# Six of eight norms' last step on GpSimd, row sums of the banded softmax on VectorE, and new order lists

## The chip, the cores and the metric

The kernel runs on one core of one Trainium2 chip. The metric is the device time of one launch in microseconds (us). Of the kernel before, three runs gave 1738.55, 1740.66 and 1747.6 us; the median is 1740.66 us. Everything is one program with hand-placed semaphores: TensorE (PE), VectorE (DVE), ScalarE (ACT), GpSimd (POOL) and the DMA queue of SyncE (SP) each work through a list of their own, in order.

## The reference, cut to what matters

Eight batches of 512 tokens by 128 features go through four blocks (gated attention with a selective scan, a feed-forward block, a 16-head attention, two layers of local attention with 8 heads and a window of 64). Each block stands between two layer norms without weights:

```python
def _layernorm(x, axis=-1, eps=1e-05):
    m = jnp.mean(x, axis=axis, keepdims=True)
    v = jnp.var(x, axis=axis, keepdims=True)
    return (x - m) / jnp.sqrt(v + eps)

x = L0_attn_x                                   # (8, 512, 128)
x = x + _layernorm(_L0_attn_ref(_layernorm(x)))  # norms 0 and 1
x = x + _layernorm(_L0_ffn_ref(_layernorm(x)))   # norms 2 and 3
x = x + _layernorm(_L1_attn_ref(_layernorm(x)))  # norms 4 and 5
x = x + _layernorm(_L1_ffn_ref(_layernorm(x)))   # norms 6 and 7
```

In the local attention each block of 64 queries sees 128 keys, and the softmax runs over those:

```python
sim = jnp.einsum('bhwid,bhwjd->bhwij', bq, bk)
mask = (i < j) | (i > j + WINDOW) | (j == -1)
sim = jnp.where(mask, -jnp.finfo(sim.dtype).max, sim)
attn = jax.nn.softmax(sim, axis=-1)
out = jnp.einsum('bhwij,bhwjd->bhwid', attn, bv)
```

## The kernel before, in words

**Tiling.** A batch lies in SBUF as 128 tokens (partitions) by 4 blocks of 128 features: one tile of 128x512. Four batches are in flight at a time, each with its own set of 18 such tiles ("streams"); batch 4 takes the buffers of batch 0 once that has finished, and so on.

**Units.** The work of a batch is cut into named units, each on one engine. `network()` (line 93) lists them. Those that matter here:

- Scan (S6) of 16 states in 8 steps m: ACT makes the decays (`da`, L1484), DVE multiplies (`dbu`, L1113), scans twice (`h`, L1119) and multiplies (`hc`, L1123), PE adds up (`y_sum`, L673). Two spreading DMAs feed each step.
- A norm k of 8: DVE `ln_stats` (L1308, L1311), ACT `ln_rstd` (L1442, L1444, a logarithm and an exponential), DVE `ln_shift` (L1316, minus mean times rstd, 128x4), then ACT `ln_apply` (L1632), four activations of 128x128 with scale and bias. Norms 3 and 5 read PSUM, the other six SBUF. `LN_ON_SCALAR` (line 156) holds all eight, so the other branch, `ln_normed` on DVE, is not used.
- Local attention, 2 layers by 4 blocks of 128 tokens per batch, so 64 times in all: among others `l_bias` on DVE (L1242, maxima), `l_exp` on ACT (L1591, eight activations of 128x128 from PSUM, one per head, each with an `accum_out` that leaves the row sum in `lsum`), `l_inv` on DVE (L1251, reciprocal of 128x8), `l_probs` on POOL (L1765, the probabilities times these), `lp_turn` on PE (L602). POOL also does `qk_sum` (L1754) and `k_rot` (L1760) there.
- Row maxima of the 16-head attention: PE `row_scores`, DVE `row_max` (L1197), 22 per batch.

**Table loads.** ACT's functions live in tables. `table(name)` emits a load (L1425) when the last one loaded was another. Logarithm and exponential share one table, Silu and Tanh another, Gelu has a third.

**Order.** No engine chooses at run time. `ORDER` holds one string for each engine; three characters stand for a unit (the batch, with 8 for preparation, and the unit's number in base 36), `BANKS` gives PE's PSUM banks. `orders()` decodes them, and each engine issues its units in that sequence, waiting on semaphores where a unit needs another's result.

Of the kernel before, what the change touches and what calls it, by code (L numbers as in the profile page):

```python
# [16 lines left out]
P = 128  # L17
# [75 lines left out]
def network():  # L93
# [62 lines left out]
LN_ON_SCALAR = (0, 1, 2, 3, 4, 5, 6, 7,)  # L156
# [33 lines left out]
def begins(name, args):  # L190
# [6 lines left out]
        "10080010110200010300100200380130030110410530220030300420120220300510610700600730430510820420510900800930630710a20620710c"  # L197
        "10b10f10e10d00a00c10g00b00f00e00d30810h00g10i10j30900h00i00j20810k30a10l10n10p10m10o10q30c10r00k30b00l00n00p00m00o00q30f"
        "30e00r10s30d10t10u10w10v20c20920a20b30g00s20f00t00u00w00v20e20d30h30i30j20g10y10x10z11211011111f11e11g11d11c11b11h11i11a"
        "11411911711511611311800y00x11j00z01001201101f01d01g11k11l11n01e11m11o11q11s11p11v11r11w11t01c11u11y01h11x11z121123120126"  # L200
        "12212712401b30k01i12512912812a12c12e30l12b12d12h12i12f01430n01a12g12k12j12l12n12p30p12m12o01701512q01930m12r01601330o12s"
        "01830q12t20h30r01j20i20j01k01l01n01m01o12u01q01p12v01r12w13501s30s01v01t01w30t30u01u01x12x01y01z02112y13402002212z02330v"
        "02402602730w02502913620k02802a13713d13113002b13802c13202d13e20l02e02i20n13f02f02h13313a13913g02j13m13h02g02l02k13b02m13n"
        "13c20p02n20m02p20o02o02q13o30y13j13i13p02r30x13q13k02s30z13l02t31231020q31131f20r13s13r31g13t31d31e02u13u31b31c13v02w02v"
        "13w03531h13x20s31i31a20t31414214314014113y13z02x02y03414402z20v31931714503614714614g03103003703d03803203e03314831314914f"
        "14a03f31520u03a03903g20w14h03m03h14b14c14i14o14j14d14p03b03o14e03p03n03j03i31614q03c31820y14k14l14r14x14s14m14y14n03q03k"
        "31j20x03l14z20z14u14t21215014v15103s03r14w03t21031k31l31n03u21103v15315231m03w15403x15531o31q15604204315704004103y03z158"
        "31p04415b15c04515d15e15915a04615f04704g31r31s31v31w31t21f21d04831u04904f31x04a31y31z32032132332632204h32432721e21g04c04b"
        "04i04o04j04d04p32804e32550032950132a32c32e04q32b32i32d04k04l04r04x04s32f04m04y04n32g32h32k50221b32j04z32l32n04u04t32m050"
        "04v32o05104w32p21h50332q21c21i21a21432r21721632s05305221921532t05421305521805605705805b05c05d05e05905a32u50405f32v32w335"  # L210
        "21j50550632x32y33432z21k50721l21n21m33621o21q33721p33133021r33d33821s50821t21v50940021u33221w33e21y33321x33f21z401402220"
        "33g33m33a33933h50a33b33n33c22140322333o22222422622733p22550b22833j33i50f50c33q50e22a33k50d22933l22b22c50g22d22e40422i22h"
        "22f22g22k33s33r22j22l40522m22n22p33t22o22q50h33u22r50i33v40650j33w22s40733x22t40834234334034133y33z40934440a34522u34622v"
        "34740c34g40b22w23540f40e34840d50k22x50l50n50p40g34934f34a50m50o50q22y23422z50r34h40h34c40i34b34i34o40j34j23023123623734d"
        "23d34q34p34r34e34x23823234k34l23e34m34s34y50s34z35034n23f23350t50u50w23923a23g23m34t34u35150v34v23b23n40k34w23c40l40n40p"
        "40m40o40q23h35235323o23p35440r35523j35623i23q35750y50x23k50z51051251123l51f40s35823s23r40t40u40w35b35c35d35e35935a40v51d"
        "35f51e51g51h23t51b23u51c23v51i23w51a23x51451551624224324024123y23z51351951724451840y40x24540z51j41024770024670170251k51l"
        "24g70351n51m51o51q51s24851p51r51v51w51t24924f51u51y51x51z52152052352252452652724a52552952852a52c24h52b52e52h52d70424b24c"
        "52f70552g52i52k24i24d52j52l24p70652m52n52p24o52o52q24j70752r41224e70841141f52s52t70970a24k24l24q24r24x24s41g24m70b70c52u"
        "70f70e70d41e24z24y25041d24n24t24u70g25152v41b52w53541c24v70h41h70i41i41441a24w70j25225352x52y53452z419416415417413536254"  # L220
# [12 lines left out]
        "74c74b44q44r63s63r74d63t74j63u74p63v74q74r74x63w74e44x44d63x44k74k74l44l74m74y64264364064163y63z74s64474z75074n64544s646"
        "64764g74t74u75144z45074v44p44e74w44m44t44u45164844y44n75375264964f44v45264a45375444w75545464h75664i64o75764b64c64j64d64p"
        "64e75845564q45664r64x45764k64l64s64m64y64n75b75c75d64z75e65075975a64t64u45865164v75f64w45b45c65265345d65445e65545965645a"
        "65745f65865b65c65d65e65965a65f"),
    "DVE": (
        "10000080280080510100110200280710380300380180680410410510600410700500680900780820030020120230130210830310910a20310b10c10d"
        "10e10f00800900a00b00c30400d00e30500f30610g30710h10i20410j10k20510l10m20610n00g20700h00i00k00j00l00m00n30830930a30b30c30d"
        "30e30f10o10q10p10r20820920a20b20c20d20e20f10s10t10u10v00o00q00p00r00s00t00u00v30g30h30i30j30k30l30m30n10w10x10y10z20g20h"  # L240
        "20i20j20k20l20m20n11011211111300w00x00y00z01001201111401311530o30q11630p30r11730s01401530t30u01611830v20o01711920q11a018"
        "30w11b20p20r11c30x11d01911e30y01a30z01b31020s01c31201d31101e31320t11f11g11h20u20w20v11i20x11j20y20z11k01f11l01g01h11m210"
        "21221101i21301j11n11o11p01k11q31401l31501m31631701p01n01q01o21431821531921611s11t11r11w11u12912812a12712612512b12c11v11y"
        "12312111z12012411x12212d01s01r01t01w02902702a01u01v21702831a31b02631c12e31d02b31e02502c12f01y02412g02101z31f12h02331g020"
        "01x31h02202d12i31i12j21831j12k12l31k21912m31l21a31m21b12n12o12p21c21d02e31n31o21e12t12q12u31p31q12r02f12y12v12z12w12s133"
        "02g13013412x13121f21g31s02h31r13531t13202i31w13602j21h32902k31u02l21i02m32a21j32732802n13721k32513821l32621m31v02o32b02p"
        "13932c31y32413c13b13a02t02u13d02q13e21p32321q32102r13f13g02y02v02z02s31x02w13k13h13l21n31z13i21o03303003413p13m03113q13j"
        "13n32002x32232d21s13u13r13v03513o13s21r03221t03621w13w13t21u13x03721v03813y03913z03c03b03a14003d14203e14314103f03g144145"
# [141 lines left out]
def build(nc, x_d, colp_d, rowp_d, wts_d, ints_d, cst_d, pre_d, tab_d, bcst_d, ones_d, out_d):  # L390
    ctx = ExitStack()
    with ctx:
# [16 lines left out]
        def at(name, *args):  # L409

            return sem(name), value[batch[0], name, args]
# [132 lines left out]
        def normed_at(k):  # L544
            return at("ln_apply" if k in LN_ON_SCALAR else "ln_normed", k)

# [1431 lines left out]
```

## Time and profile before

| | |
|---|---|
| median of three runs | 1740.66 us |
| the profiled execution | 1741.72 us, its span 1739.9 us |
| PE busy | 1434.9 us (82%) |
| ACT busy | 1268.0 us (73%) |
| DVE busy | 1254.2 us (72%) |
| POOL busy | 367.3 us (21%) |
| table loads on ACT | 124, 159.1 us |
| DMA queue 1 | 24.5% of 16 engines' span |

Busy time counts overlapping instructions of an engine once, so it can be less than the count times the mean. The mean granted TensorE clock is 0.924 of full speed.

### The profile page before, as it was taken

How to read it: one execution, taken by the hardware profiler on the slowest of the kernel's cores; microseconds unless marked ns; L12 is line 12 of the kernel's file. 1: busy time of each engine (PE TensorE's matmuls, PEld its weight loads, DVE VectorE, ACT ScalarE, POOL GpSimd, SP SyncE). 2: the span in 40 equal slices, each digit the busy share in tenths (PEclk: the TensorE clock that was granted, in tenths of full speed). 3: DMA queues.
4: the chain of work that ended last, by engine and by line, in shares of the span. 5: the costliest groups of instructions: out<-in, count | busy, mean ns of one | idle time of the engine just before them, and what ended most of it. 6: DMA issues, size and time to landing. Idle time of an engine off the chain costs nothing.

```text
span 1739.9 us, 32913 instructions
## 1 busy us (share of the span) xinstructions
PE 1434.9 (82%) x13044; PEld 849.7 (49%) x13044; DVE 1254.2 (72%) x2201; ACT 1268.0 (73%) x2878; POOL 367.3 (21%) x222
## 2 busy tenths in 40 slices
PE   3667697889888998888889887789798898988986
PEld 1122454345556554445456534555345564656664
DVE  6999978565886549968786878764977685477554
ACT  5523792779668787787798484878588985898875
POOL 2000000003144130410252021221003451045440
PEclk8776996899999999899999998989899998999998
DMA  7774224013023012323003433003320140000100
GB/s 250 232 242 138 73 76 98 3 26 74 11 52 60 23 39 84 117 81 121 19 19 81 92 105 103 16 9 88 106 98 17 24 94 10 10 17 20 31 20 19
DMA packets 70985, 121.75 MB, mean 70 GB/s; under 512 B 6864, under 2 KB 28112, under 8 KB 69072
## 3 DMA queue, kind: packets, MB, share of 16 engines
q1 hardware_dynamic: 70832, 119.65, 24.5%
q8 instruction: 104, 1.70, 0.4%
q14 instruction: 49, 0.40, 0.1%
HBM read 89.34 MB, written 15.60 MB: 60 GB/s over the span
## 4 chain that ended last, share of the span: by engine, by line
PE 36%; ACT 28%; DVE 28%; issue 5%; DMA 1%; POOL 0%; SPq 0%; ACTq 0%; DVEq 0%; POOLq 0%
ACT tiles L1591 8%; ACT L1425 5%; PE psum L602 5%; DVE neg_max L1197 5%; DVE tiles L1119 5%; PE psum L848 4%; DVE tiles L1113 2%; DVE tiles L1123 2%; PE psum L880 2%; ACT tiles L1535 2%; ACT tiles L1632 2%; PE psum L881 2%; PE psum L833 2%; PE psum L980 2%; PE psum L947 2%
## 5 line engine op out<-in xcount | busy, mean ns | idle before, releaser
L1754 POOL TENSOR_TENSOR tiles<-tiles 128x1024 f32<-128x1024 f32 x64 | 155.1, 2424 | 669.7 <-DVE tiles L1376 669.7
L602 PE MATMUL psum<-cst,tiles 128*128 128x128 f32 x1408 | 211.4, 287 | 87.9 <-DVE tiles L1337 32.6
L602 PEld LDWEIGHTS psum<-cst,tiles 128*128 128x128 f32 x1408 | 163.3, 146 | 164.9 <-issue 102.5
L1591 ACT ACTIVATE tiles<-psum,lmax,invn 128x128 f32<-128x128 f32 x512 | 226.3, 470 | 15.2 <-DVE lmax L1247 11.8
L1197 DVE TENSOR_REDUCE neg_max<-psum 128x2 f32<-128x1024 f32 (+3 forms) x176 | 189.8, 1117 | 32.5 <-PE psum L800 32.3
L673 PE MATMUL psum<-tiles,cst 128*128 128x512 f32 x256 | 152.4, 728 | 43.1 <-DVE tiles L1123 43.1
L1765 POOL TENSOR_TENSOR tiles<-tiles,lsum 128x1024 f32<-128x1024 f32 x64 | 126.9, 1983 | 280.7 <-DVE lsum L1251 280.7
L1425 ACT ACT_TABLE_LOAD x124 | 159.1, 1283 | 2.9 <-PEq L1968 0.7
L1119 DVE TENSOR_TENSOR_SCAN tiles<-tiles 128x512 f32<-128x512 f32 x128 | 157.2, 1259 | 2.7 <-ACT tiles L1484 0.5
L1484 ACT ACTIVATE tiles<-tiles,colp 128x512 f32<-128x512 f32 x128 | 90.3, 719 | 87.3 <-DVE tiles L1119 79.1
L1232 DVE TENSOR_REDUCE ssq<-tiles 128x16 f32<-128x1024 f32 x64 | 77.8, 1215 | 86.3 <-ACT tiles L1680 86.0
L800 PE MATMUL psum<-bcst 64*128 64x128 bf16 x2048 | 138.9, 229 | 0.0
L1535 ACT ACTIVATE tiles<-psum 128x768 f32<-128x768 f32 (+1 forms) x128 | 115.0, 927 | 27.2 <-PE psum L800 23.5
L800 PEld LDWEIGHTS psum<-bcst 64*128 64x128 bf16 x2048 | 102.8, 101 | 30.8 <-issue 7.8
L848 PE MATMUL psum<-tiles 128*32 128x512 f32 (+3 forms) x1024 | 99.5, 472 | 19.6 <-ACT tiles L1535 12.0
L1591 ACT ACTIVATION_READ_ACCUMULATOR tiles<-psum,lmax,invn 128x1 f32 x512 | 111.9, 219 | 0.0
L673 PEld LDWEIGHTS psum<-tiles,cst 128*128 128x128 f32 x256 | 52.6, 222 | 119.0 <-DVE tiles L1123 69.9
L812 PE MATMUL psum<-tiles 48*128 48x384 bf16 (+3 forms) x512 | 82.1, 335 | 34.3 <-DVE neg_max L1197 19.2
L1242 DVE TENSOR_REDUCE lmax<-psum 128x8 f32<-128x1024 f32 x64 | 77.8, 1216 | 25.0 <-PE psum L917 25.0
L1680 ACT ACTIVATE tiles<-psum 128x1024 f32<-128x1024 f32 x64 | 66.0, 1034 | 40.7 <-PE psum L881 40.6
L833 PE MATMUL psum<-tiles 51*128 51x256 bf16 (+3 forms) x512 | 75.9, 313 | 23.7 <-ACT tiles L1535 7.5
L1113 DVE TENSOR_TENSOR tiles<-tiles 128x1024 f32<-128x1024 f32 x64 | 88.0, 1376 | 0.0
(226 smaller groups left out, 3324.4 us busy)
## 6 DMA issues: line engine op xcount, KB each, us to landing
tiles<-bc_scratch SPq DMA_DIRECT2D x128, 512.0 KB, 4.8
v_prev<-tiles SPq DMA_DIRECT2D x112, 128.0 KB, 2.3
split_scratch<-tiles SPq DMA_DIRECT2D x96, 128.0 KB, 2.4
tiles<-split_scratch SPq DMA_DIRECT2D x32, 384.0 KB
wts<-in_wts SPq DMA_DIRECT2D x1, 3114.0 KB, 15.8
tiles<-in_x SPq DMA_DIRECT2D x8, 256.0 KB, 3.8
out<-tiles SPq DMA_DIRECT2D x8, 256.0 KB, 2.7
tiles<-in_rowp SPq DMA_DIRECT2D x1, 768.0 KB, 7.4
```

The source lines that it names most:

```text
L602: ins = nc.tensor.transpose(ps[:, j * 128:(j + 1) * 128], src[:, j * 128:(j + 1) * 128], ident)
L673: ins = mm(place("y_sum", m), ident, T(S6_H[m % 3] + a), start=False, stop=(m == STATES // 2 - 1 and a == 1))
L800: ins = mm(out, bconst("ident_sw" if swap else "ident")[r], bconst(mask + "_sw" if swap else mask)[r], start=False, stop=swap)
L848: ins = mm(ps[32 * c:32 * c + 32, jk * 128:512], values_ext()[:, jk, a:a + 32], head_probs(jk, i)[:, e, :], start=(jk == 0), stop=(jk == N ...
L1113: tt(two(S6_H[m % 3]), two(S6_H[m % 3]), T(DTU).unsqueeze(1).to_broadcast([P, 2, SEQ]), ALU.mult).then_inc(sem("dbu"), 1)
L1119: nc.vector.tensor_tensor_scan(T(t), T(S6_DA[n % 3]), T(t), 0.0, ALU.mult, ALU.add).then_inc(sem("h"), 1)
L1197: nc.vector.tensor_reduce(nm[:, j, :, i * n:(i + 1) * n], ps.rearrange("p (e n) -> p e n", e=2)[:, :, 0:n * keys].rearrange("p e (a n) -> ...
L1425: nc.scalar.preload_act_table_set(name)
L1535: ins = fn(head_probs(jk, i), ps[:, :, 0:w], ACT.Exp)
L1591: ins = fn(pr[:, i * 128:(i + 1) * 128], ps[:, i * 128:(i + 1) * 128], ACT.Exp, bias=own(lmax)[:, b, i:i + 1], scale=own(invn)[:, j, 0, 2 ...
L1754: tt(T(TURNED, 2), T(TURNED, 2), T(TURNED + 2, 2), ALU.add).then_inc(sem("qk_sum"), 1)
L1765: tt(pr, pr, own(lsum)[:, j % 2, :].unsqueeze(2).to_broadcast([P, LHEADS, 128]), ALU.mult).then_inc(sem("l_probs"), 1)
```

## The change

The last step of norms 0, 1, 2, 4, 6 and 7 goes to GpSimd: a product of the 128x512 tile with the broadcast `rstd`, a wait on its own semaphore, and a sum with the broadcast `shift`. Norms 3 and 5, whose input is in PSUM, stay on ACT. `l_exp` no longer asks for row sums; `l_inv` computes them with one reduction over 128x8x128, waits for it, and takes the reciprocal. All five order strings and the banks are new. PE keeps its 1570 units, DVE its 1226 and SP its 204; ACT goes from 1394 to 1346, POOL from 202 to 250.

```diff
 def normed(k):
-    return [("ACT", "ln_rstd", k)] + ([("DVE", "ln_shift", k), ("ACT", "ln_apply", k)] if k in LN_ON_SCALAR else [("DVE", "ln_normed", k)])
+    return [("ACT", "ln_rstd", k), ("DVE", "ln_shift", k), ("ACT" if k in LN_ON_SCALAR else "POOL", "ln_apply" if k in LN_ON_SCALAR else "ln_scaled", k)]
...
-LN_ON_SCALAR = (0, 1, 2, 3, 4, 5, 6, 7,)
+LN_ON_SCALAR = (3, 5)
...
 ORDER = {
...
+    (five new strings)
...
 def l_inv(l, j):
     dve.wait_ge(*at("l_exp", l, j))
+    step(nc.vector.tensor_reduce(own(lsum)[:, j % 2, :], T(LP, 2).rearrange("p (i n) -> p i n", n=128), AX.X, ALU.add))
+    settle()
     nc.vector.reciprocal(own(lsum)[:, j % 2, :], own(lsum)[:, j % 2, :]).then_inc(sem("l_inv"), 1)
...
     ins = fn(pr[:, i * 128:(i + 1) * 128], ps[:, i * 128:(i + 1) * 128], ACT.Exp,
-             bias=own(lmax)[:, b, i:i + 1], scale=own(invn)[:, j, 0, 2 * g + e:2 * g + e + 1],
-             accum_out=own(lsum)[:, b, i:i + 1])
+             bias=own(lmax)[:, b, i:i + 1], scale=own(invn)[:, j, 0, 2 * g + e:2 * g + e + 1])
...
+def ln_scaled(k):
+    pool.wait_ge(*at("ln_shift", k))
+    to = blocks(T(LN_TO[k]))
+    each = lambda v: v[:, k, :].unsqueeze(2).to_broadcast([P, NJ, 128])
+    steps[0] += 1
+    tt(to, blocks(ln_in(k)), each(own(rstd)), ALU.mult).then_inc(sem("pool_step"), 1)
+    pool.wait_ge(sem("pool_step"), steps[0])
+    tt(to, to, each(own(shift)), ALU.add).then_inc(sem("ln_scaled"), 1)
```

## Rows read from the trace of the kernel before

**Rows 1.** Page: busy us, share of the span, instructions
```profile
span 1739.9 us, 32913 instructions
PE 1434.9 (82%) x13044; PEld 849.7 (49%) x13044; DVE 1254.2 (72%) x2201; ACT 1268.0 (73%) x2878; POOL 367.3 (21%) x222
```
**Rows 2.** Windows: stretch, length, busy us of PE, PEld, DVE, ACT, POOL; PEclk, DMA
```profile
87.00:174.00 87.00, 58.96 (x97) 20.57 (x95) 82.91 (x72) 28.66 (x38) 0.00 (x0) 0.72 0.57 190
...
0.00:348.00 348.00, 237.35 (x1245) 116.57 (x1245) 280.36 (x463) 194.87 (x333) 12.15 (x18) 0.81 0.44 139
...
0.00:1035.00 1035.00, 830.73 (x7008) 474.43 (x7009) 782.94 (x1368) 726.28 (x1572) 180.21 (x115) 0.91 0.31 87
1035.00:1740.00 705.00, 604.14 (x6037) 375.31 (x6035) 471.28 (x834) 541.76 (x1306) 187.06 (x107) 0.94 0.17 45
```
**Rows 3.** Page: the chain that ended last, by engine and by line
```profile
PE 36%; ACT 28%; DVE 28%; issue 5%; DMA 1%; POOL 0%; SPq 0%; ACTq 0%; DVEq 0%; POOLq 0%
ACT tiles L1591 8%; ACT L1425 5%; PE psum L602 5%; DVE neg_max L1197 5%; DVE tiles L1119 5%; PE psum L848 4%; DVE tiles L1113 2%; DVE tiles L1123 2%; PE psum L880 2%; ACT tiles L1535 2%; ACT tiles L1632 2%; PE psum L881 2%; PE psum L833 2%; PE psum L980 2%; PE psum L947 2%
```
**Rows 4.** Chain, 95 to 112 us: start us, us, what (the scan)
```profile
100.73 2.35 DVE tiles L1119 x2
...
105.50 2.35 DVE tiles L1119 x2
```
**Rows 5.** Chain, 1340 to 1370 us: shares by line, then pieces
```profile
by line: ACT tiles L1591 23.2%; ACT tiles L1632 20.1%; ACT L1425 17.1%; ACT tiles L1680 6.1%; ACT tiles L1674 5.6%; issue 4.0%; ACT tiles L1553 3.9%; PE psum L602 3.7%; ACT tiles L1569 3.6%; ACT tiles L1576 3.2%; ACT lnv L1442 3.1%; ACT rst
...
1342.26 2.92 ACT tiles L1632 x8
...
1358.28 1.28 ACT L1425
1359.57 0.01 issue
```
**Rows 6.** Page: the group of table loads
```profile
L1425 ACT ACT_TABLE_LOAD x124 | 159.1, 1283 | 2.9 <-PEq L1968 0.7
```
**Rows 7.** Timeline of ACT, 1148 to 1160 us: start us, us, instruction
```profile
1149.27 0.46 ACT L1591 ACTIVATE tiles<-psum,lmax,invn 128x128 f32<-128x128 f32 x1
1149.63 0.19 ACT L1591 ACTIVATION_READ_ACCUMULATOR tiles<-psum,lmax,invn 128x1 f32 x1
1149.72 0.45 ACT L1591 ACTIVATE tiles<-psum,lmax,invn 128x128 f32<-128x128 f32 x1
...
1152.67 0.23 ACT L1591 ACTIVATION_READ_ACCUMULATOR tiles<-psum,lmax,invn 128x1 f32 x1
1152.91 1.28 ACT L1425 ACT_TABLE_LOAD   x1
```
**Rows 8.** Timeline of ACT, 1167 to 1171 us
```profile
1167.10 1.50 ACT L1632 ACTIVATE tiles<-psum,shift,rstd 128x128 f32<-128x128 f32 x4
```
**Rows 9.** Timeline of DVE, 1680 to 1684 us: a reduction and its follower
```profile
1680.42 1.22 DVE L1232 TENSOR_REDUCE ssq<-tiles 128x16 f32<-128x1024 f32 x1 [0.22 <-ACT tiles L1680]
1681.67 0.18 DVE L1235 TENSOR_SCALAR ssq<-ssq 128x16 f32<-128x16 f32 x1
```
**Rows 10.** POOL and DVE operations by line: ns min/median/max, first and last start
```profile
L1760 POOL TENSOR_TENSOR tiles<-tiles,invn x64: 1034/1042/1904, 385.0 to 1686.9; 128x512 f32<-128x512 f32 x64
L1345 DVE TENSOR_TENSOR tiles<-tiles x8: 691/692/2731, 34.7 to 1239.6; 128x512 f32<-128x512 f32 x8
L1113 DVE TENSOR_TENSOR tiles<-tiles x64: 1192/1216/3360, 46.3 to 1293.1; 128x1024 f32<-128x1024 f32 x64
L1242 DVE TENSOR_REDUCE lmax<-psum x64: 1172/1216/1226, 392.3 to 1696.4; 128x8 f32<-128x1024 f32 x64
```
**Rows 11.** Page: groups of DVE operations; busy us, mean ns after the first bar
```profile
L1113 DVE TENSOR_TENSOR tiles<-tiles 128x1024 f32<-128x1024 f32 x64 | 88.0, 1376 | 0.0
...
L1197 DVE TENSOR_REDUCE neg_max<-psum 128x2 f32<-128x1024 f32 (+3 forms) x176 | 189.8, 1117 | 32.5 <-PE psum L800 32.3
```
**Rows 12.** Tile lsum: who waited for it (us, times)
```profile
  POOL tiles L1765: 280.7, 40
  PEld psum L602: 9.8, 14
```

More of the change, by code:

```diff
@@ L201 @@
[L201 to L208, printed above, removed]
@@ L312 @@
[L312 to L318 removed]
+        "80010000010110200100210300380110400410520030020120200530130210620330300610700710800810920420530400910a30500a10c10b10e10f"
@@ new lines @@
+    "POOL": (
+        "80180010000020030010110200100210310400300420120230130210510610720320430330410910a10810c10d10b10f10g10e10h00500600700900a"
+        "10i10j00800c00d10l10m10k00b00f00g10o10p10n00e10r10s10q00h10t00i00j10u00l00m00k50000o00p00n00r00s00q00t20500u206207400209"
+        "20a20820c20d20b20f20g20e20h30530630730930a30820i30c20j30d30b20l20m20k30f30g30e20o20p20n30h20r20s20q20t30i30j50130l30m502"
+        "30k20u30o30p60030n30r30s40130q50340230t50440340430u70060160260360450570170260550650770370460660760960a60850950a60c60d60b"
+        "50860f60g60e50c50d60h40550b50f50g60i60j60l60m60k60o60p60n60r60s60q40640760t50e40940a40850h70540c40d40b60u70670740f40g40e"
+        "70970a70840h70c70d70b70f70g70e50i50j70h50l50m50k50o50p50n50r50s40i40j50q70i70j40l40m40k50t70k70l70m40o40p40n70o70p70n40r"
+        "40s40q70r70s70q40t70t50u70u40u"),
@@ new lines @@
+    "SP": (
+        "10000080480180680780880080280580380980a20080b101001300102002103003104004105005201106301006107202203302007108303008109204"
+        "20530400930520620730630720820930830910a10b10c00b10d00a10e00c10f10g00d00e20a20b10h20c10i30b30a30c00f00g10j10k00h10l00i10m"
+        "00j20d00k20e10n50000l00m50150250330d30e50420f20g00n40050550650750840120h40220i40350930f30g40440520j40620k30h40730i20l408"
+        "20m40930j30k60020n30l60160230m60360460560660750b50a60860950c40b40a40c30n70070170270350d70450e70570670770860a60b70960c60d"
+        "60e40d40e50f50g60f60g70a70b70c60h60i50h70d70e60j60k50i40f40g60l60m70f70g60n40h40i70h70i50j50k50l40j40k70j70k50m70l40l70m"
+        "40m50n70n40n"),
@@ L329 @@
[L329 to L332 removed]
+    "012102010101232423232340454400410400010145104402401120101204125400102146024026646464640624624670676002402035035720346024"
@@ new lines @@
+    "620436016351653106301640540460253620525702325207245025201500101350605631640160104506341601241246146701401357137571410735"
+    "025350543240570245650365065562061652345310323420246706740121046010143062224501641023201363450453420234574257010350730472"
+    "076764760613057107127127017017010734610603024646402407245701074731541631413613164301643704670104601460176247624002461014"
+    "134601267347602460624724726024502042602604040460260340343603623230120302151211001211010101034030102321056061765357122252"
@@ L335 @@
+    "735270620742040272673047035707370572705325317573715707152046204546021047651073707570107140654357120147041040234757420727"
+    "472305724342353243054304737434703701760130767501707440570470513056507012034632716214516752761057450726547546076524760161"
+    "04023627010767040301605405304630120136732027657601737107156367657457645765675767665475675675675677")
 class Waiting:
@@ L544, in normed_at @@
         def normed_at(k):
-            return at("ln_apply" if k in LN_ON_SCALAR else "ln_normed", k)
+            return at("ln_apply" if k in LN_ON_SCALAR else "ln_scaled", k)
         def ln_in(k):
@@ L1317, in ln_shift @@
                         op1=ALU.mult).then_inc(sem("ln_shift"), 1)
-                def ln_normed(k):
-                    dve.wait_ge(*at("ln_rstd", k))
-                    for j in range(NJ):
-                        ins = ts(T(LN_TO[k])[:, j * 128:(j + 1) * 128], ln_in(k)[:, j * 128:(j + 1) * 128], own(mv)[:, k, j, 0:1],
-                                 own(rstd)[:, k, j:j + 1], ALU.subtract, ALU.mult)
-                    ins.then_inc(sem("ln_normed"), 1)
                 def mean_sq():
@@ L1390, in _ @@
                             "y1": y1, "shift2_b": shift2_b, "f_norm": f_norm, "hh": hh,
-                            "y_next": y_next, "out": out, "skip": skip_matrix, "hidden_bias": hidden_bias, "scaled_w1": scaled_w1, "ln_shift": ln_shift, "ln_normed": ln_normed, "qk_turned": qk_turned})
+                            "y_next": y_next, "out": out, "skip": skip_matrix, "hidden_bias": hidden_bias, "scaled_w1": scaled_w1, "ln_shift": ln_shift, "qk_turned": qk_turned})
             @block.scalar
@@ L1765, in l_probs @@
                     tt(pr, pr, own(lsum)[:, j % 2, :].unsqueeze(2).to_broadcast([P, LHEADS, 128]), ALU.mult).then_inc(sem("l_probs"), 1)
-                run("POOL", {"v_zero": v_zero, "dbu": dbu, "hc": hc, "ve_ones": ve_ones, "k_rot": k_rot, "l_probs": l_probs, "qk_sum": qk_sum, "bias_split": bias_split})
+                run("POOL", {"ln_scaled": ln_scaled, "v_zero": v_zero, "dbu": dbu, "hc": hc, "ve_ones": ve_ones, "k_rot": k_rot, "l_probs": l_probs, "qk_sum": qk_sum, "bias_split": bias_split})
             @block.sync
```

230 lines of the change are left out of this document (108 added, 122 removed).

## The prediction

> **What bounds the kernel now.** I read the busy totals first. PE is busy 1434.9 of 1739.9 us; ACT (1268.0) and DVE (1254.2) are level with each other and each idle for more than a quarter [rows 1]. No engine is full over the span, so the time is PE's work plus 305 us in which PE waits. Then the windows, to see where. In the first 348 us PE is busy 237 us, so 111 us are lost there, while DVE is busy 280; from 87 to 174 us DVE is busy 82.9 of 87 [rows 2]. That start belongs to the scans on DVE: a step m begins every 4.77 us (100.73 to 105.50) with no gap, 38 us for a batch's eight [rows 4]. The other 194 us of PE's idle time lie after 348 us, where neither DVE nor ACT is full. Then the chain that ended last: PE 36%, ACT 28%, DVE 28% [rows 3]. PE does its 1435 us mostly beside the chain; the chain runs through whichever engine holds the next result. On ACT it runs chiefly through two things this change touches: the exponentials L1591 (8%, 139 to 142 us) and the table loads L1425 (5%, some 92 us; the page rounds) [rows 3]. From 1340 to 1370 us it stays on ACT nearly throughout: L1591 23.2%, norm steps L1632 20.1%, table loads 17.1% [rows 5]. So ACT is a bound in stretches, though not over the whole span.
>
> **Fewer table loads.** Walking ACT's list and loading where the function's table changes gives 124 loads before, as the trace counts [rows 6], and 81 after. At 1.283 us each, 43 fewer take 55.2 us off ACT. Of the 159.1 us of loads 92 are on the chain, a share of 0.58: 55.2 x 0.58 = 32 us. Bounds: nothing (all the removed ones lay beside the chain) and 55.
>
> The trace shows a load that starts 0.01 us behind the last accumulator read (ends 1152.90, load 1152.91) and is followed 0.01 us after its end by "issue" and the next activation [rows 5, 7]. The Trainium skill, "ScalarE: Activation LUTs", section "What ACT_TABLE_LOAD costs", adds a drain of about 1.38 us to each, 2.66 us together. By that page 43 loads would be 114 us of ACT time and the term on the chain about 66 us instead of 32. The trace speaks against it, and the sum keeps the row's 1.283.
>
> **No accumulators.** An exponential with an accumulator begins every 0.45 us (1149.27, 1149.72), and a set of eight ends at 1152.90, 3.63 us after its start [rows 7]. The accumulator read (0.19 to 0.23 us) half hides under the next activation, so the removed reads are worth less than their durations. Four activations of the same shape without one take 1.50 us [rows 8], so eight take 2.92 in the row of x8 [rows 5]: 0.7 us saved in each of 64, 45 us of ACT. On the chain are 140 of 64 x 3.63 = 232 us, a share of 0.6: 27 us. Bounds: 0 and 45.
>
> **Norms.** 48 applications at 1.46 us (2.92 for two [rows 5]) leave ACT: 70 us. L1632 holds 2% of the chain (some 32 us), three quarters of it moved norms, so 24 us go. In their place POOL runs two 512-column operations with a broadcast operand; its nearest row is L1760, 1042 ns [rows 10], so 2 x 1.04 + 0.1 = 2.2 us per norm. POOL rises by 106 us to 473, still 27% of the span. What was on the chain because ACT was full vanishes; where the norm's own reader is next, 2.2 us stand for 1.5. I take half and half: 8 of 16 norms on the chain return with 2.2, 18 us. Net gain 6; bounds -10 (all 48 latencies longer by 0.7, a third on the chain) and +24. Queued behind a waiting ln_scaled are l_probs, k_rot and qk_sum of other batches, on which PE waits; the bounds take that in.
>
> POOL also slows DVE. DVE operations with two SBUF tensors sometimes wait for a POOL operation: L1345 691/692/2731 ns, L1113 up to 3360, while the reduction from PSUM never passes 1226 [rows 10]. L1113's mean is 1376 against its median of 1216 [rows 10, 11], 10 us over 64, and with the other such lines I estimate 24 us in all beside 367 us of POOL. 100 us more of POOL bring 7 by that ratio, at most 100 if each of the 96 blocked DVE for its 1.04. The Trainium skill says the same in "GPSIMD Engine Reference", section "Specifications", row "SBUF interfaces": they are shared with VectorE, with contention where it has two SBUF inputs. By the rule alone, each overlap with such an operation would cost; the rows agree in kind, and set the size.
>
> **Row sums on DVE.** One reduction over 128x1024 from SBUF takes 1.22 us and its follower starts 1.25 us after it began [rows 9]. 64 x 1.25 = 80 us more for DVE: 1254 + 80 + 7 = 1341. As latency it costs l_inv 1.25 against 0.7 won in l_exp; but l_probs behind l_inv is hardly on the chain (POOL 0% [rows 3]; POOL itself sits idle 280.7 us until lsum, PE behind it only 9.8 us of weight loads [rows 12]). As load it counts more: DVE's 28% of the chain are 487 us of its 1254, a share of 0.39, and 87 x 0.39 = 34 us lost. Bounds: 0 and 87.
>
> **The new order** moves everything else, which no row prices. I look at how much DVE and PE must have done at a point deep in the lists, the third y_sum of batch 7. By counting units and weighting them with the line means, PE has 828 us of its 1435 before it; DVE must have gone through 59 of 64 scan steps, 32 of 64 local-attention blocks and 114 of 176 row maxima. What it has left then is 32 x 7.3 for the blocks, 62 x 1.08 for the maxima [rows 11], 5 x 4.77 for scans and some 95 for the rest, 420 us; so 1341 - 420, say 920, stand before it. The kernel before had done 831 of PE and 783 of DVE at 1035 us, and needed 705 us for the rest [rows 2]. The new order thus asks DVE for 137 us more in the same stretch, and leaves a lighter second part (DVE 420 against 471, ACT without its share of 170).
>
> **The sum.** -32 - 27 - 6 + 34 = -31 us by the chain. By the two stretches: if DVE works at 0.90 up to the point (it was 0.81 in the first 348 us and 0.95 from 87 to 174 [rows 2]), it is reached at 1022 us; PE's 607 us after it at 0.89 instead of the present 604/705 = 0.86 take 682. 1704. The chain gives 1741.7 - 31 = 1711. I take 1707 for the profiled execution, 1706 beside the median, which stands 1 us below it.
>
> **Rivals.**
> - *A, ACT was worse than the chain shows.* The old order has loads in clusters (three within 30 us at 1340 [rows 5]), and once ACT's delay is gone, PE waits less everywhere. ACT then loses 170 us, to 1098, at a share of 0.58: 99 less 34 for DVE, 65 us. 1677 us. For: the 194 us that PE loses behind 348 us, with no engine full. Against: other chains lie close beside this one.
> - *B, the other side: DVE becomes the bound before the last scans.* The order asks 920 us of DVE before that point. Below 920/1035 = 0.89 of DVE use, it comes later than now. At 0.85 it comes at 1082; with the rest at 0.89, 682 us, that makes 1764 us. For: the old kernel used DVE at only 783/1035 = 0.76 there, and l_inv now waits in DVE's queue where ACT had room. Against: DVE idled because it had to wait for PE and ACT, and scans run back to back without either.
> - *C, no change.* The start is DVE's and stays (PE's 111 us), PE's 1435 stay; the relief on ACT falls into waits that DVE's load replaces: chain bounds of 30 us won and 30 lost, 1740.
> - *D, POOL blocks DVE*: norms 0, 1 and 2 of one batch stand beside the scans of another, the operations with two SBUF tensors. Half of the 96 blocking for 1.04 us would be 50 us of DVE, by 0.39 another 20 less 3: 1724. It shifts the forecast, not its sign.
>
> **Numbers.** Half a percent, 8.7 us, is about what can be told from no change here. Forecast with its own spread 0.38, A 0.22, D 0.07, C 0.14, B 0.19. Faster 0.68 (forecast, A, D, and a little of C), same 0.12, slower 0.20. The range 1655 to 1760 leaves out A's far end and B's.
>
> **What would show it.** ACT busy 1268 - 55 - 45 - 70 = 1098 us with 81 loads; L1591 x8 in 2.9 us and no accumulator reads; DVE about 1341, its new reduction at 1.22 us; POOL about 473 with the new lines at 1.04. PE's idle time before the last scans and L1113's mean against its median tell B and D from the forecast. Wrong would be the forecast if L1425 and L1591 keep their shares of the chain, or if DVE's busy share before that point stays below 0.89.

## The result, and the profile after

The changed kernel takes 1736.14 us (median of 8, 1734.12 to 1740.94) against 1744.08 us (8 runs, 1738.55 to 1747.6): a ratio of 0.9963, with its 95% interval [0.9945, 0.998]. That is 0.4% faster: the interval leaves out 1, but the gain is smaller than the half percent that the prediction asked of a change. The forecast was 1706 us, with a range of 1655 to 1760.

The profiled execution took 1740.27 us. Its page, with span, busy us, share and instructions of each engine, and then the chain that ended last, by engine and line:

```profile
span 1738.5 us, 32317 instructions
PE 1423.2 (82%) x13044; PEld 852.0 (49%) x13044; DVE 1331.7 (77%) x2265; ACT 1100.3 (63%) x2131; POOL 488.3 (28%) x318
...
PE 37%; DVE 31%; ACT 20%; issue 6%; POOL 3%; DMA 2%; SPq 1%; POOLq 0%; DVEq 0%; ACTq 0%
ACT tiles L1586 9%; DVE tiles L1119 5%; DVE neg_max L1197 5%; PE psum L602 5%; PE psum L848 3%; DVE tiles L1113 3%; DVE tiles L1123 2%; PE psum L673 2%; ACT tiles L1530 2%; PE psum L980 2%; PE psum L880 2%; PE psum L972 2%; PE psum L833 2%; DVE ssq L1232 2%; PE psum L881 2%
...
L1757 POOL TENSOR_TENSOR tiles<-tiles 128x1024 f32<-128x1024 f32 x64 | 154.2, 2410 | 376.6 <-DVE tiles L1371 376.6
L1751 POOL TENSOR_TENSOR tiles<-tiles,rstd 128x512 f32<-128x512 f32 x48 | 62.9, 1310 | 684.9 <-DVE shift L1318 684.6
...
L1586 ACT ACTIVATE tiles<-psum,lmax,invn 128x128 f32<-128x128 f32 x512 | 185.9, 478 | 17.1 <-DVE lmax L1247 16.9
...
L1251 DVE TENSOR_REDUCE lsum<-tiles 128x8 f32<-128x1024 f32 x64 | 78.0, 1219 | 73.9 <-ACT tiles L1586 73.8
...
L1420 ACT ACT_TABLE_LOAD x81 | 103.9, 1283 | 2.1 <-PEq L1971 0.7
```

Against [rows 1, 3, 6] the work moved as written: 81 loads instead of 124, ACT 168 us less, DVE 78 us more, POOL 121 us more. The loads have left the list of the chain's lines, where they had 5%. But the exponentials kept theirs: L1591 had 8%, its successor L1586 has 9%, though each set is 0.7 us shorter. ACT's share fell from 28 to 20%; most of it went to DVE and POOL (28 to 31%, 0 to 3%).

PE does the same 13,044 matmuls, in 1423.2 instead of 1434.9 us busy. It idles 315.3 us, more than the 305.0 of before. The windows tell where (columns as in [rows 2]):

```profile
0.00:348.00 348.00, 225.60 (x1202) 116.89 (x1206) 284.71 (x476) 166.39 (x281) 52.23 (x46) 0.85 0.45 139
0.00:1035.00 1035.00, 813.19 (x6841) 479.06 (x6842) 829.85 (x1378) 632.02 (x1210) 280.20 (x182) 0.91 0.29 86
1035.00:1738.00 703.00, 610.03 (x6204) 372.90 (x6203) 501.88 (x888) 468.32 (x921) 208.07 (x136) 0.94 0.19 46
0.00:1137.00 1137.00, 893.98 (x7339) 523.23 (x7339) 917.90 (x1538) 679.02 (x1293) 292.20 (x194) 0.90 0.31 89
1137.00:1738.00 601.00, 529.24 (x5705) 328.73 (x5705) 413.83 (x728) 421.32 (x839) 196.06 (x124) 0.97 0.14 34
```

By 1035 us PE has done 6841 matmuls, 167 fewer than before [rows 2], though ACT had 94 us less to do by then. In the rest it does 6204 in 703 us where 6037 took 705. What the second part wins, the first has lost.

The chain from 1340 to 1370 us, where ACT stood nearly throughout in [rows 5], now shows in small what came in place of the accumulators (start us, us, what):

```profile
1343.43 0.47 issue
1343.90 2.91 ACT tiles L1586 x8
1346.83 1.23 DVE lsum L1251
1348.08 0.20 DVE lsum L1253
1348.29 0.15 DVE tiles L1258
1348.44 1.14 DVE neg_max L1197
1349.58 0.79 DVE stats L1310 x4
```

The set of eight is 0.7 us shorter, and the reduction that follows puts 1.23 us on the chain, ahead of a row maximum and a norm's statistics. Summed over 30-us windows of the chain, L1586 holds 167 us of it (L1591 before: 142), the loads 23 (95), the reduction 23, and POOL's L1751, L1757 and L1768 some 35 (POOL had 0% before [rows 3]).

VectorE waits for the exponentials more than before, too. The row sums stand at the head of its list until L1586 is done: its waits there are these, over the whole span (us in all, times, longest us):

```profile
DVE lsum L1251 <- ACT tiles L1586: 73.8, 57, 3.5
```

In the kernel before the same place, with the reciprocal alone, held 44.7 us in 32 waits.

### The profile page after: what moved, and what is told of

It is laid out like the page before. It is cut to its first block, busy times and chain, and to the rows that moved or that the text cites. A ratio compares the mean times of both kernels' runs of the same rounds, so it can differ in the third digit from the quotient of the medians.

```text
span 1738.5 us, 32317 instructions
## 1 busy us (share of the span) xinstructions
PE 1423.2 (82%) x13044; PEld 852.0 (49%) x13044; DVE 1331.7 (77%) x2265; ACT 1100.3 (63%) x2131; POOL 488.3 (28%) x318
## 4 chain that ended last, share of the span: by engine, by line
PE 37%; DVE 31%; ACT 20%; issue 6%; POOL 3%; DMA 2%; SPq 1%; POOLq 0%; DVEq 0%; ACTq 0%
ACT tiles L1586 9%; DVE tiles L1119 5%; DVE neg_max L1197 5%; PE psum L602 5%; PE psum L848 3%; DVE tiles L1113 3%; DVE tiles L1123 2%; PE psum L673 2%; ACT tiles L1530 2%; PE psum L980 2%; PE psum L880 2%; PE psum L972 2%; PE psum L833 2%; DVE ssq L1232 2%; PE psum L881 2%
## 5 line engine op out<-in xcount | busy, mean ns | idle before, releaser
L1757 POOL TENSOR_TENSOR tiles<-tiles 128x1024 f32<-128x1024 f32 x64 | 154.2, 2410 | 376.6 <-DVE tiles L1371 376.6
L1751 POOL TENSOR_TENSOR tiles<-tiles,rstd 128x512 f32<-128x512 f32 x48 | 62.9, 1310 | 684.9 <-DVE shift L1318 684.6
L1197 DVE TENSOR_REDUCE neg_max<-psum 128x2 f32<-128x768 f32 (+3 forms) x176 | 189.4, 1117 | 27.8 <-PE psum L800 27.3
L1586 ACT ACTIVATE tiles<-psum,lmax,invn 128x128 f32<-128x128 f32 x512 | 185.9, 478 | 17.1 <-DVE lmax L1247 16.9
L673 PE MATMUL psum<-tiles,cst 128*128 128x512 f32 x256 | 143.6, 690 | 45.8 <-DVE tiles L1123 45.7
L1768 POOL TENSOR_TENSOR tiles<-tiles,lsum 128x1024 f32<-128x1024 f32 x64 | 128.5, 2007 | 171.2 <-DVE lsum L1253 171.2
L1119 DVE TENSOR_TENSOR_SCAN tiles<-tiles 128x512 f32<-128x512 f32 x128 | 163.2, 1301 | 1.4
L1251 DVE TENSOR_REDUCE lsum<-tiles 128x8 f32<-128x1024 f32 x64 | 78.0, 1219 | 73.9 <-ACT tiles L1586 73.8
L800 PEld LDWEIGHTS psum<-bcst 64*128 64x128 bf16 x2048 | 102.1, 100 | 31.8 <-issue 10.9
L812 PE MATMUL psum<-tiles 48*128 48x512 bf16 (+3 forms) x512 | 82.5, 338 | 33.1 <-DVE neg_max L1197 23.8
L848 PE MATMUL psum<-tiles 128*32 128x512 f32 (+3 forms) x1024 | 93.3, 451 | 3.8 <-ACT tiles L1586 2.2
```

The lines of the kernel that those rows point to most:

```text
L673: ins = mm(place("y_sum", m), ident, T(S6_H[m % 3] + a), start=False, stop=(m == STATES // 2 - 1 and a == 1))
L800: ins = mm(out, bconst("ident_sw" if swap else "ident")[r], bconst(mask + "_sw" if swap else mask)[r], start=False, stop=swap)
L848: ins = mm(ps[32 * c:32 * c + 32, jk * 128:512], values_ext()[:, jk, a:a + 32], head_probs(jk, i)[:, e, :], start=(jk == 0), stop=(jk == N ...
L1119: nc.vector.tensor_tensor_scan(T(t), T(S6_DA[n % 3]), T(t), 0.0, ALU.mult, ALU.add).then_inc(sem("h"), 1)
L1197: nc.vector.tensor_reduce(nm[:, j, :, i * n:(i + 1) * n], ps.rearrange("p (e n) -> p e n", e=2)[:, :, 0:n * keys].rearrange("p e (a n) -> ...
L1586: ins = fn(pr[:, i * 128:(i + 1) * 128], ps[:, i * 128:(i + 1) * 128], ACT.Exp, bias=own(lmax)[:, b, i:i + 1], scale=own(invn)[:, j, 0, 2 ...
```

## The experiments

Two theories stood first. Theory O: the new order lists failed, and each operation is a gain or neutral at its place. Theory L: DVE's greater load ate the gain. A third possibility is that GpSimd's part (latency, contention with DVE) eats it. Ratios are to the kernel before, with their 95% intervals; "us" behind them are the ratio, or the difference of two ratios, times 1744. One ratio is good to 3 to 6 us, a difference of two to 5 to 8.

### Order and operations apart

`e4_new_order_alone`: the new strings with the old operations, the six norms' units set into ACT's string.

```diff
 ORDER = {
-    (five old strings)
+    (five new strings, the six norms' units on ACT)
```

> The new order lists with the old operations: all eight norms on ScalarE, each at the place in time where GpSimd did it, row sums in ScalarE's accumulators, 81 table loads. Theory L: the order is a gain by its 43 fewer table loads (32 us by the chain) and VectorE is 80 us lighter: 1700 to 1720. Theory O: the order is worth nothing or is worse than the old one, 1740 to 1765, as it was laid out for other operations.

Measured 1799.3 us, 1.0299 [1.0274, 1.0324]. The order alone costs 52 us, more than either theory allowed; on it, the new operations win 59 (1.0299 to 0.9963). Where the six norms go in ACT's list is a choice of this run (the times at which GpSimd did them), and part of the 52 may be that choice.

`e5_new_order_accum`: the changed kernel with accumulators instead of the reduction.

```diff
-    step(nc.vector.tensor_reduce(own(lsum)[:, j % 2, :], ...
-    settle()
...
+             accum_out=own(lsum)[:, b, i:i + 1])
```

> The changed kernel with the row sums back in ScalarE's accumulators; the new order and the norms on GpSimd stay. It prices the row sums in the new order. Theory L: 15 to 35 us faster than the changed kernel, 1700 to 1720. Theory O: within 5 us of the changed kernel, 1731 to 1741, or slower.

Measured 1781.27 us, 1.0204 [1.0176, 1.0232]. So in this order the norms on POOL win 17 us (against e4), and the sums on DVE 42 (e5 to after), though they take 80 us of DVE for 47 of ACT. Of e5, the busy line and who waited for L1584, its exponentials (us in all, times, longest us):

```profile
PE 1431.9 (80%) x13044; PEld 858.6 (48%) x13044; DVE 1251.7 (70%) x2201; ACT 1147.4 (65%) x2643; POOL 487.6 (27%) x318
...
PE psum L880 <- ACT tiles L1584: 19.1, 9, 3.5
...
PE psum L602 <- ACT tiles L1584: 16.9, 11, 2.8
```

The same two waits of the changed kernel:

```profile
PE psum L880 <- ACT tiles L1586: 11.6, 9, 2.1
...
PE psum L602 <- ACT tiles L1586: 9.5, 11, 2.1
```

The waits are as many, and on average longer by 0.8 us (7.5 over 9) and 0.7 (7.4 over 11), about what a set is longer: in this list PE comes to these points no later than the short exponentials end, and pays for the whole difference. The two waits together are 15 us of the 32 by which PE idles less in the changed kernel (346.9 to 315.3).

`e1_old_order_sums`: the kernel before, with the reduction for the accumulators.

```diff
+    step(nc.vector.tensor_reduce(own(lsum)[:, j % 2, :], ...
+    settle()
...
-             accum_out=own(lsum)[:, b, i:i + 1])
```

> The kernel before with one edit: the row sums of the banded softmax by VectorE (64 reductions of 128x1024, 1.22 us each, and no accumulators on ScalarE); the old order lists and the norms on ScalarE stay. Theory L (VectorE's load is what ate the gain: its use before the last scans was 0.81 where 0.90 was forecast, so 80 us more for it cost more than 45 us less for ScalarE win): slower than before by 10 to 35 us, 1750 to 1775. Theory O (the new order lists are what failed; each operation is a gain or neutral at its place): within 5 us of before, 1735 to 1745. My sum by shares of the chain (27 won, 31 lost) says +4, beside theory O.

Measured 1753.46 us, 1.0059 [1.0039, 1.008]: 10 us lost, in theory L's range, by the edit that wins 42 in the new order. Its chain by engine:

```profile
PE 38%; DVE 36%; ACT 19%; issue 3%; POOL 1%; DMA 1%; SPq 0%; ACTq 0%; DVEq 0%; POOLq 0%
```

ACT 28 to 19%, DVE 28 to 36% [rows 3]: the place on the chain changes hands, and the sum stays.

`e3_old_order_both`: e1 with the six norms on POOL as well, in the places in time where ACT had them.

```diff
-LN_ON_SCALAR = (0, 1, 2, 3, 4, 5, 6, 7,)
+LN_ON_SCALAR = (3, 5)
```

> The kernel before with both edits of the operations: row sums on VectorE and the last step of six norms on GpSimd, placed in GpSimd's list where ScalarE had done them in time; the order of PE, VectorE, SyncE and of the rest of ScalarE as before, 124 table loads. Against the run with the sums alone it prices the norms. Theory L: norms 0 to 10 us won, so 5 to 30 us slower than before, 1745 to 1770. Theory O: 5 to 15 us faster than before, 1727 to 1737, and faster than or level with the changed kernel (1736), since the new lists would add nothing.

Measured 1772.18 us, 1.0149 [1.0124, 1.0174], 16 us above e1. All the operations of the change cost 26 us in the old order and win 59 in the new one. Theory O falls, since the operations lose in the old order; theory L and GpSimd's part fall as general answers, since the sums win 42 us and the norms 17 in the new one. In these four combinations no edit has a value of its own.

### Work taken out

`e6_before_no_accum`, `e7_after_no_reduce`, `e9_before_no_loads` and `e8_after_no_loads` leave work out, to price it; all four compute other values than the reference. `accum_out` goes in e6, the reduction in e7, and both then take the reciprocal of the row maxima:

```diff
-    nc.vector.reciprocal(own(lsum)[:, j % 2, :], own(lsum)[:, j % 2, :])
+    nc.vector.reciprocal(own(lsum)[:, j % 2, :], own(lmax)[:, j % 2, :])
```

> The kernel before, old order, with the accumulators left out and no reduction in their place (VectorE takes the reciprocal of the row maxima instead, so the row sums are left out): ScalarE loses its 45 us and nothing is added. It prices the first half of the row sums' move. Theory S (a removed microsecond is worth its share of the chain, 0.6): 27 us faster than before, 1716. Theory P (several chains run close together, and the next one takes over): under 12 us faster, 1731 to 1743. With the run of the sums alone (1753) it also gives the price of the reduction: 37 us by S, 10 to 22 by P.

> The changed kernel with the reduction left out (reciprocal of the row maxima instead): VectorE loses 80 us, 1.25 in each of 64 blocks, and ScalarE keeps its short exponentials. Theory S: 80 us at VectorE's share of the chain (31% of 1738 over 1332 us, 0.40), 32 us faster than the changed kernel, 1704. Theory P, as the accumulators' return cost 45 us although VectorE was relieved of the same 80: 0 to 12 us faster, 1724 to 1736, and ScalarE and PE are what it waits for.

And e9 (old order) and e8 (new order) need one table only:

```diff
-    table(SILU)
-    fn(T(MX), ..., ACT.Silu)
+    table(LNEXP)
+    fn(T(MX), ..., ACT.Identity)
```

> The kernel before with one table load instead of 124, by the same replacement: 158 us off ScalarE. Theory S: the chain holds 92 us of loads, so 92 us faster, 1651. Theory P: 30 to 60 us faster, 1683 to 1713. A third of either (43 of 124) is what the order's count of loads could have brought by itself: 32 by S, 10 to 20 by P.

> The changed kernel with one table load instead of 81 (Silu, Tanh, Gelu and Sigmoid replaced by Identity, which changes the values and not the work): 103 us off ScalarE. Theory S: loads are no longer among the chain's first 15 lines, so under 2% of 1738, under 35 us faster, 1705 to 1725. Theory P: under 20, 1716 to 1736. If loads were still what holds it, 60 (a share of 0.58): 1676.

| | removed | ratio | worth |
|---|---|---|---|
| e6, old order | accumulators, ACT -41 us | 0.9911 [0.9885, 0.9938] | 15.5 us |
| e7, new order | reductions, DVE -77 us | 0.9915 [0.9892, 0.9937] | 8 us from after |
| e9, old order | 123 loads, ACT -158 us | 0.962 [0.9595, 0.9646] | 66 us |
| e8, new order | 80 loads, ACT -104 us | 0.9893 [0.9869, 0.9917] | 12 us from after |

From e6 to e1, DVE's 80 us of reductions cost 26: the forecast's terms were 27 won and 34 lost, measured are 15.5 and 26. Theory P's range held in e7 and e8; for the reduction in the old order it did not quite (26 for 10 to 22). The accumulators (15.5) and the loads of the old order (66) lie between what S and P said. In the new order the loads hurt by 12 us instead of 66. That is 54 us less, more than the forecast's 32. But free of loads, the old order with its operations is at 1678 us and the new one at 1727. The busy line of e9, and then of e8:

```profile
PE 1414.2 (84%) x13044; PEld 842.0 (50%) x13044; DVE 1255.7 (75%) x2201; ACT 1109.6 (66%) x2755; POOL 367.8 (22%) x222
```

```profile
PE 1421.9 (82%) x13044; PEld 855.2 (50%) x13044; DVE 1334.2 (77%) x2265; ACT 996.0 (58%) x2051; POOL 488.2 (28%) x318
```

In e8 PE idles 305 us (span 1727.2) beside engines at 77, 58 and 28%. What holds it there is neither loads nor an engine that is full.

### Work put in

`e10_before_32_more_loads`: one more load of the same table ahead of every second `l_exp` of the kernel before.

```diff
 def l_exp(l, j):
+    if j % 2:
+        nc.scalar.preload_act_table_set(LNEXP)
```

> The kernel before with one more table load (of the table that is already there, 1.283 us) ahead of the exponentials of every second block of 128 tokens: 32 in all, 41 us added to ScalarE at L1591's place, next to the 45 us whose removal gained 15. Theory F (a list is fitted to its durations; work that is added is on the chain more often than the same work removed was worth): 30 to 50 us slower than before, 1774 to 1794. Theory S (a share of the chain, 0.6 or what e6 showed, 0.34): 14 to 25 us slower, 1758 to 1769.

Measured 1791.41 us, 1.0269 [1.0243, 1.0295]. The group of the added loads and the chain by engine:

```profile
L1581 ACT ACT_TABLE_LOAD x30 | 38.5, 1283 | 0.5
...
PE 37%; ACT 32%; DVE 23%; issue 5%; DMA 1%; POOL 1%; SPq 0%; ACTq 0%; DVEq 0%; POOLq 0%
```

The trace has 30 of the 32 that were expected. The two that lack belong to blocks where a load of L1425 ends just before the exponentials, which follow it by 0.01 us, so those two did not run. 38.5 us of work cost 47 us, as theory F had it. It is not only waiting: of the 51 us between the two profiled spans, 18 are PE's busy time (1434.9 to 1453.3) at a lower granted clock (0.924 to 0.914), and 32 its idle time.

`e11_after_reduce_twice`: the reduction of the changed kernel, done twice.

```diff
+    step(nc.vector.tensor_reduce(own(lsum)[:, j % 2, :], ...
+    settle()
```

> The changed kernel with the row sums' reduction done twice (the same result): VectorE gains 80 us where leaving the reduction out won 8. Theory F: 25 to 60 us slower than the changed kernel, 1762 to 1797. Theory S, by the share that e7 showed (0.1): 8 us slower, 1745.

Measured 1794.66 us, 1.0275 [1.0247, 1.0302]: 54 us more than the changed kernel for some 74 of DVE (1405.7 us busy). Taking the first 77 out won 8. This too is in theory F's range.

So the time doesn't answer in proportion. At the exponentials of the old order a microsecond taken out is worth 0.37 us (e6) and one put in costs 1.2; a microsecond of loads taken out anywhere in it is worth 0.42; a microsecond of reduction taken from the new order 0.11, put in 0.7. That is what many chains of nearly the same length do, each engine's list being issued in a fixed sequence: take from one, and the next holds the time; add to one, and it grows nearly in full. (The 1.2 is more than full; the slower clock has its share in it.) It is a reading of these numbers, not shown by a run of its own. I call it the fit of the lists to the durations.

### Lists laid anew

If the fit sets the time, other lists should move it by some per cent with no operation changed. For six kernels I laid the lists anew: on each engine the units of one batch keep their sequence, and only how the batches interleave changes, and with it PE's banks. The sequence kept is that of the kernel before in f2, g4 and g1, and that of the changed kernel in f1, g3 and g2, so some of the order differs between the two groups besides the interleaving. The lists came out of a search over interleavings, with the traces' median durations for each unit, 1.3 us per load and the measured landings of the DMAs.

```diff
 ORDER = {
-    (five strings)
+    (five strings, found for this set of operations)
```

> The changed kernel's operations with order lists laid out anew: on each engine only the interleaving of the four streams is changed (units of one stream keep their sequence), and PE's banks, by a search that replays the lists with each unit's median duration from the two traces, 1.3 us per table load and the measured landings of the DMAs. Theory F (the time is set by how the lists fit the durations, more than by the sum of work on any engine; the changed kernel's 315 us of idle PE are mostly a matter of order): 1615 to 1660, 80 us or more below 1736. Theory W (the wait chains through ScalarE, VectorE and GpSimd are inherent in the operations, and an order can move them about but not shorten them): no more than 15 us faster, 1720 or above.

> The kernel before with its own operations (norms on ScalarE, accumulators) and order lists laid out anew by the same search for the same time. Against f1 it prices the change of the operations when each has an order of its own. Theory F: 1600 to 1650, level with or below f1, as the operations are worth within 15 us of each other once the order fits them. If the operations are a gain in themselves and only the old lists hid it, f1 is faster than f2 by 20 us or more.

> Row sums on VectorE, norms on ScalarE, lists laid out for these operations by the search that made f1 and f2. If the sums' move is the harmful half (VectorE has become the longest chain, 40% of it in f1): slower than f2 (1690) by 10 us or more. If the operations do not matter once the lists fit: 1680 to 1700.

> Six norms' last step on GpSimd, accumulators on ScalarE, lists laid out for these operations by the same search. If the norms' move is the harmful half (a step 0.7 us longer, and waits of VectorE behind GpSimd): 1700 or more while g1 stays below it. If the operations do not matter: 1680 to 1700.

> The changed kernel's operations with a second list, found from f1's by replaying with small random delays added to the units. If the chip's unevenness is what parts the replay from the measured time, this list is faster than f1 (1699) by 10 us or more; else within 10 us of it.

> The old operations with a second list from another run of the same search, with 78 table loads (f2 has 92). It shows the search's spread: within 20 us of f2's 1690, on either side. If the table loads decided, 5 to 10 us faster than f2.

| | operations | loads | us | ratio |
|---|---|---|---|---|
| f2 | as before | 92 | 1689.52 | 0.9681 [0.9656, 0.9706] |
| g4 | as before, second list | 78 | 1730.13 | 0.992 [0.9894, 0.9946] |
| g1 | sums on DVE | 99 | 1682.23 | 0.9634 [0.9604, 0.9665] |
| g2 | norms on POOL | 87 | 1712.26 | 0.9823 [0.9789, 0.9857] |
| f1 | both | 90 | 1698.92 | 0.9735 [0.9709, 0.976] |
| g3 | both, second list | 82 | 1685.82 | 0.9666 [0.9636, 0.9696] |

All six are faster than both kernels, g4 by 0.8% with the very operations of before. Order alone is thus worth some 3%. But the search had promised more: theory F's 1615 to 1660 us for f1 and 1600 to 1650 for f2 came out as 1699 and 1690, so neither F nor W held for f1. Two lists for one set of operations differ by 41 us (f2, g4; within 20 was expected) and 13 us (f1, g3). Between the sets the best lists found lie at 1690, 1682, 1712 and 1686 us, within that spread: what the operations are worth by themselves can't be told from six lists. g2 alone, above 1700 with g1 below it, would have spoken against the norms' move; f1 and g3, which have it too, are at 1699 and 1686. Loads don't order the table either: the fewest, 78, have the slowest kernel, the most, 99, the fastest. The fastest, g1, is 3.7% below the kernel before and by ratio 3.3% below the changed one. Its busy line and a window of it that sets beside [rows 2]:

```profile
PE 1412.3 (84%) x13044; PEld 841.3 (50%) x13044; DVE 1312.2 (78%) x2265; ACT 1193.6 (71%) x2341; POOL 362.5 (22%) x222
```

```profile
0.00:348.00 348.00, 238.38 (x1367) 126.64 (x1367) 288.97 (x517) 198.44 (x352) 12.14 (x18) 0.84 0.44 139
...
0.00:1035.00 1035.00, 847.22 (x7280) 489.45 (x7280) 844.55 (x1446) 714.26 (x1372) 183.89 (x118) 0.92 0.32 93
```

By 1035 us it has done 7280 matmuls and 845 us of DVE; the changed kernel 6841 and 830, the kernel before 7008 and 783. In the first 348 us, which I had taken for DVE's and fixed, it already does 1367 matmuls against 1245 and 9 us more of DVE. PE's busy time there is the same, though (238 us against 237), so those are mostly short matmuls, at a granted clock of 0.84 against 0.81, and the 111 us that PE lost at the start are still lost.

## Why the prediction was wrong

**The work on each engine was near.** ACT 1098 us forecast, 1100.3 measured; 81 loads of 1.283 us; a set of exponentials in 2.91 us; DVE 1341 against 1331.7; POOL 473 against 488.3; the reduction at 1.22 us. L1751 has its 1.04 us only as a median. A small misreading: 17.1% of the 30 us in [rows 5] are four loads, not three.

**The step that failed is the one from work to time.** "By the two stretches: if DVE works at 0.90 up to the point" had the third y_sum of batch 7 at 1022 us. It starts at 1137 us in the changed kernel, and at 1046 before. DVE has 917.9 us of work before it, as forecast (920), but was used at 917.9/1137 = 0.81: the 0.90 stood between two rows and came from neither. PE had done 894 us by then and not 828, so my count of PE's units was off by 66 us. The first error makes the point 115 us later, the second leaves less work behind it and makes the rest 81 us shorter (601 for 682); what remains, 34 us, is the whole miss of this sum (1704 against the span of 1738). PE's use in the rest went as forecast, 529 of 601 us, 0.88 for 0.89. DVE's largest single wait before the point is the new one: 35.3 us in 29 waits of the row sums for the exponentials, where the kernel before had 14.8 in 16 up to its own point. The forecast had no term for this wait when it let DVE work at 0.90. With DVE's use below 0.89 and the exponentials still on the chain, both signs that the prediction itself named against its forecast have come.

**The sum by the chain** priced each term as if its share of the chain would go or come with it. The accumulators were worth 15.5 us for 27, the reductions cost 26 for 34, the loads of the old order were worth 66 for the 92 that they held on it. These are sizes. The norms, put at 6 won, cost 16 in the old order and win 17 in the new: there not even the sign is one number. The larger error lay in adding them up for a new order that "no row prices" as though it were neutral. It costs 52 us with the old operations (e4). That term, put at nothing without a reason, is larger than the whole gain forecast. The chance I had given to C was 0.14; what C says (30 won and 30 lost) is close to what came, with amounts larger on both sides: 54 won on the loads' price, 48 given back in all that is left without them (1678 to 1727).

**Rivals.** A fell with e9: without any load the old order reaches 1678, and ACT's 158 us bring 66, not 0.58 of them. B named the right place: DVE's use fell below 0.89 and the point came late, by 91 us. But its price was wrong, as PE had done 66 us more by then and had less left. Yet DVE is no bound: 77 us less of it bring 8 (e7). D is real, though smaller than its 50 us. Two pairs differ in little but the norms: DVE's busy time rises by 23.1 us (e1 to e3: 1328.1 to 1351.2) and by 22.2 (e4 to e5: 1229.5 to 1251.7), where I had put 7, and D 50.

**DVE's sum, closed.** 1254.2 before, -24.7 by the order alone (e4), +22.2 by POOL's norms (e5), +80.0 by reductions: 1331.7. My 1341 had the first at nothing and 7 for the second, so it came near by two errors of opposite sign. The order term is inferred from one pair of traces.

## What to carry to other kernels

Where every engine issues a fixed list and none is full, busy time and shares of the chain don't price an edit: here work taken out was worth between a quarter and three quarters of its share (8 us for 31, 66 for 92), and work put in cost 0.7 to 1.2 us for each us. Price the list and the operations apart, one run for the new order with the old operations and one for the reverse; here they were +3.0% and +1.5%, and together -0.4%. And before an operation is moved for a few per cent, lay the lists anew for the operations that are there, more than once, since one list says little (1690 and 1730 us for the same work).

## What the runs showed of the hardware

**GpSimd and VectorE hold each other up, both ways.** The line of the new product on POOL, ns min/median/max and first and last start:

```profile
L1751 POOL TENSOR_TENSOR tiles<-tiles,rstd x48: 1038/1040/4208, 17.6 to 1732.9; 128x512 f32<-128x512 f32 x48
```

Its mean of 1310 is a quarter above its median, and the 1.04 us of the forecast came out as 2.5 us for the pair of operations instead of 2.1. One of the 48, at 683.21 us, lasts 4.21 us while DVE runs a scan, a product and another product of two SBUF tensors one behind the other (L1119, L1113, L1123) in their usual 1.2 us each; GpSimd is through 0.9 us behind the last. On DVE, the 22 to 23 us of the two pairs of runs are not mainly the scan steps: L1113, L1119 and L1123 together have 9.5 of them (e1 to e3) and 9.3 (e4 to e5). The rest is spread over small operations, such as eight products of 128x4 that go from 2.0 to 7.1 us. What the scan steps show is how much the order matters. In the changed kernel:

```profile
L1119 DVE TENSOR_TENSOR_SCAN tiles<-tiles 128x512 f32<-128x512 f32 x128 | 163.2, 1301 | 1.4
...
L1113 DVE TENSOR_TENSOR tiles<-tiles 128x1024 f32<-128x1024 f32 x64 | 87.8, 1376 | 0.0
```

and in g1, with the same work on DVE, another order and 126 us less on POOL:

```profile
L1119 DVE TENSOR_TENSOR_SCAN tiles<-tiles 128x512 f32<-128x512 f32 x128 | 153.1, 1224 | 5.6 <-ACT tiles L1486 2.7
L1113 DVE TENSOR_TENSOR tiles<-tiles 128x1024 f32<-128x1024 f32 x64 | 78.6, 1233 | 3.4 <-DMA tiles<-bc_scratch 2.9
```

The kernel before had 1376 for L1113 with no norm on POOL [rows 11]: what stands beside the scans counts, not only how much POOL does. f1 has 1228 with all six norms on POOL. The Trainium skill, "GPSIMD Engine Reference", section "Specifications", has the two engines share their SBUF interfaces, with contention for VectorE instructions in a 2-port mode or with two SBUF inputs. The runs agree that there is contention and give the size, 22 to 23 us of DVE for 96 operations of 1.04 us.

**A table load is 1.283 us and no more.** With 123 loads gone, ACT's busy time falls by 158.4 us, 1.288 each, and the time by 66. The Trainium skill, "ScalarE: Activation LUTs", section "What ACT_TABLE_LOAD costs", would have 2.66 us for each switch, by my estimate from that figure 327 in all. The trace leaves no room for that: the next activation starts within 0.02 us of the load's end in 107 of 123 cases, and the load within 0.03 us of the instruction before it in all of them ([rows 5, 7] show one of each). Here the measurement differs from the page.

**The busy time of the same 13,044 matmuls moves** from 1409.5 us (f1) to 1453.3 (e10), 3%, with the mean granted clock at 0.952 and 0.914. The changed kernel's PE was busy 12 us less than before and idled 10 us more, at a mean granted clock of 0.926 against 0.924. Which of the two, fewer pauses or a higher clock, comes first, the runs don't tell.

**Left open:** what the operations are worth under the best list for each, and how much of what other lists gain is fewer waits and how much the clock. The 6% of issue on the changed kernel's chain (102 us) are in part a known wait: five pieces of 2.6 to 10.9 us, 36 us together, lie between 479 and 761 us, and in GpSimd's timeline each of them is L1757 waiting for DVE's L1371. The rest is in small pieces.
